# Layer norm moved into the projection stage, and half of a short filter moved from TensorE to ScalarE and VectorE

## The chip, the cores and the metric

The kernel runs on one core of one Trainium2 chip. The metric is the time of one execution in device microseconds. Before the change three runs gave a median of 2584.63 us (2580.68 to 2588.43).

## What is computed

The reference is an attention-like block with a mixture of experts behind it, for 4 sequences of 2048 tokens with 256 channels, all in float32. Only its beginning matters here:

```python
h = _layernorm(x, axis=-1) * (1 + ca) + sa
q = silu(_causal_dwconv(h @ Wq, conv_q))      # 4 taps, one filter per channel
k = silu(_causal_dwconv(h @ Wk, conv_k))
v = silu(_causal_dwconv(h @ Wv, conv_v))
beta = sigmoid(h @ Wb)                        # and sigmoid(h @ Wid + bid)
fs = _fir(v, fir_short)                       # 3 taps per channel
fl = _fir(v, fir_long)                        # 31 taps per channel
```

Behind it follow the long filter, a delta rule in chunks, the mixing of `fs`, `fl` and the delta output, and the experts. None of that is changed.

## The kernel before, in words

The program is a row of stages. Each is a block with one instruction stream per engine, and all engines meet at a barrier where one stage ends and the next begins: `setup`, `norm_inputs`, `conv_heads`, `long_filter`, `chunk_inverses`, `delta_scan`, `mix_and_experts`. Nothing orders instructions but the order in which they are written in each engine's stream and the semaphores they wait for. Every engine takes its stream strictly in that order.

The tokens are cut into 16 units of 512 (4 per sequence). `norm_inputs` works unit by unit: VectorE (DVE) takes mean and variance (`bn_stats` L312, `bn_aggr` L316, L318), GpSimd (POOL) raises the variance to the power -1/2 (L350), VectorE centers and scales (L328), TensorE (PE) turns the tile with eight transposes (L361), ScalarE (ACT) applies the modulation while it copies the result out of PSUM as `hT` (L398). TensorE then makes eight gate rows (L370), ScalarE copies them (L406), TensorE turns them back (L377) and ScalarE keeps them (L411). SyncE loads `x` and stores `hT` to `hT_d`, which a later stage reads too. At the stage's end one sigmoid runs over all gates (L416).

`conv_heads` loads `hT` again (L495) and makes, for each unit, six projection blocks of 128 channels (four of q and k, then two of v; `project`, L539). ScalarE copies each block twice: plainly into `pre` (L594) and times the last tap into `acc` (L597). VectorE adds the other three taps (`conv`, L675, three instructions per block), and ScalarE applies silu (L626). The tiles of the previous unit are meanwhile turned back to tokens on partitions: `turn_kq` (L565, four transposes) four times, and `turn_v` four times. `turn_v` makes two transposes of v (L551) and, in the same pass, the short filter as matmuls with diagonal weights: 2 channel halves times 3 taps (L555). ScalarE copies these out (`cv_k` L649, `cv_sq` L650, `cv_vf` L655), VectorE sums squares (L684), POOL makes the inverse norm (L709, L713).

All of it is written as one software pipeline by `units_ahead`: `front` does unit 0, and `body` does unit u's turns and unit u+1's projections in six slots. In slot s TensorE runs projection s, then `turn_kq` s, then `turn_v` s-1; ScalarE runs `cv_k`, `cv_sq`, the two copies of projection s, silu of block s-1 and the copy of turned v; VectorE runs the sum of squares s-1 and the filter of block s. `pj` has two buffers, so projection s waits until block s-2 has been copied out, and `acc` has three.

## Time and profile before

| what | value |
|---|---|
| median of 3 runs | 2584.63 us |
| lowest and highest run | 2580.68 and 2588.43 us |
| profiled execution: span from first to last instruction | 2587.5 us |
| profiled execution: own time | not listed apart from the span |
| busy in the span | PE 93%, PEld 64%, DVE 64%, ACT 43%, POOL 24% |
| mean granted TensorE clock | 0.946 of full speed |

The profile is one execution. PE is TensorE's matmuls, PEld its weight loads, which overlap them. A row of the timeline gives the start in us from the span's start, the duration of the merged run of equal instructions, the engine, the line, what it writes and reads, how many, and in brackets how long the engine was idle before and who ended that. Durations of neighbouring instructions overlap a little, since the next one starts before the last one's end is recorded; so the distance from one start to the next is what an instruction costs its engine when work is queued.

### The profile page before, as it was taken

Reading aid. Unit: us, or ns where it says so; the run is one execution under the profiler, and the core shown is the slowest. Engines: PE = TensorE matmul, PEld = TensorE weight load, DVE = VectorE, ACT = ScalarE, POOL = GpSimd, SP = SyncE. Lnnn points to the kernel's source line nnn. Section 1 sums busy time; section 2 is a strip of 40 time slices with the busy share of each in tenths; the row PEclk is TensorE's granted clock in tenths of the full one; section 3 lists DMA queues with packets and bytes.
Section 4 is the critical chain, followed back from the end, with each engine's and each line's share of the span. In section 5 each row is a group of like instructions: output and inputs, shape, how many; then the busy total and the mean of one; then the engine's idle time right before and its main releaser. Section 6 shows DMA issues by size and latency. Waiting matters only on the chain.

```text
span 2587.5 us, 41994 instructions
## 1 busy us (share of the span) xinstructions
PE 2394.4 (93%) x14594; PEld 1659.7 (64%) x14594; DVE 1655.0 (64%) x4354; ACT 1109.5 (43%) x2350; POOL 616.3 (24%) x417
## 2 busy tenths in 40 slices
PE   6899997667897999979999999999999999999998
PEld 4466665555676888845666666666666666666665
DVE  4487886449922566525767676667667676766675
ACT  2477876346663222224334424433443344244331
POOL 1145554031101111211312231222123132312210
PEclk9999998787667999989999999999999999999999
DMA  5447556978767767421202210220122022101000
GB/s 166 162 149 219 174 166 192 270 212 203 212 155 223 217 204 225 156 74 49 58 1 58 58 50 9 58 58 13 45 59 58 1 58 58 43 15 58 9 9 8
DMA packets 376312, 272.14 MB, mean 105 GB/s; under 512 B 199714, under 2 KB 333794, under 8 KB 373906
## 3 DMA queue, kind: packets, MB, share of 16 engines
q1 hardware_dynamic: 371474, 243.85, 33.6%
q0 software_dynamic: 4640, 25.73, 2.9%
q8 instruction: 115, 1.88, 0.3%
q14 instruction: 83, 0.68, 0.1%
HBM read 168.60 MB, written 100.93 MB: 104 GB/s over the span
## 4 chain that ended last, share of the span: by engine, by line
PE 43%; DVE 9%; issue 3%; POOL 2%; ACT 0%; DMA 0%; DVEq 0%; SPq 0%; POOLq 0%; ACTq 0%
PE mx_dn L2002 16%; PE mx_up L1988 15%; PE mx_m L1938 4%; DVE mx_acc L2316 4%; PE mx_m L1965 2%; POOL mx_rms L1894 2%; PE mx_m L1942 1%; PE mx_m L1979 1%; DVE hl L2224 1%; DVE mx_st L2214 1%; DVE hl L2199 1%; DVE hl L2188 1%; DVE mx_rms L2193 1%; PE mx_m L1973 1%; PE mx_m L1947 1%
## 5 line engine op out<-in xcount | busy, mean ns | idle before, releaser
L2316 DVE SCALAR_TENSOR_TENSOR mx_acc<-mx_dn,mx_comb,mx_acc 128x256 f32<-128x256 f32 x1024 | 424.3, 478 | 356.6 <-PE mx_dn L2002 352.7
L2002 PE MATMUL mx_dn<-mx_edn,mx_hs 128*128 128x256 f32 x2048 | 487.7, 381 | 0.0
L1988 PE MATMUL mx_up<-mx_h2T,mx_eup 128*128 128x512 f32 x1024 | 484.3, 595 | 0.0
L2002 PEld LDWEIGHTS mx_dn<-mx_edn,mx_hs 128*128 128x128 f32 x2048 | 384.4, 190 | 145.6 <-issue 91.0
L2090 ACT ACTIVATE mx_hs<-mx_up 128x512 f32<-128x512 f32 x320 | 190.8, 596 | 625.8 <-PE mx_up L1988 625.1
L1988 PEld LDWEIGHTS mx_up<-mx_h2T,mx_eup 128*128 128x128 f32 x1024 | 190.9, 190 | 156.1 <-issue 145.2
L675 DVE SCALAR_TENSOR_TENSOR cv_acc<-cv_pre,conv_w,cv_acc 128x512 f32<-128x512 f32 x288 | 215.7, 750 | 78.2 <-ACT cv_acc L597 71.3
L539 PE MATMUL cv_pj<-cv_hT,wqkv 128*128 128x512 f32 x384 | 181.8, 604 | 12.7 <-ACT cv_acc L597 7.7
L713 POOL TENSOR_TENSOR rn<-cv_ss,half_pow 128x8 f32 x64 | 127.5, 1992 | 13.2 <-POOL cv_ss L709 13.2
L1880 POOL TENSOR_TENSOR mx_st<-mx_tmp,root_pow 128x24 f32<-128x24 f32 x30 | 124.6, 4168 | 20.1 <-DVE mx_tmp L2142 20.1
L1938 PE MATMUL mx_m<-mx_hT,wr 128*128 128x512 f32 x256 | 122.2, 601 | 3.3 <-DMA mx_x<-_attn_hidden_states_dram 2.5
L1653 ACT ACTIVATE ds_U<-ds_ups 64x256 f32<-64x256 f32 x64 | 24.1, 377 | 232.2 <-PE ds_ups L1517 232.2
L2002 PEld LDWEIGHTS mx_dn<-mx_sdn,mx_hs 128*128 128x128 f32 x512 | 97.3, 190 | 40.5 <-issue 30.6
L1988 PE MATMUL mx_up<-mx_h2T,mx_sup 128*128 128x512 f32 x256 | 120.7, 605 | 2.0 <-issue 2.0
L2002 PE MATMUL mx_dn<-mx_sdn,mx_hs 128*128 128x256 f32 x512 | 121.0, 379 | 0.0
L539 PEld LDWEIGHTS cv_pj<-cv_hT,wqkv 128*128 128x128 f32 x384 | 67.6, 192 | 73.2 <-issue 54.7
L1150 PE MATMUL ci_gps<-ci_kT 64*128 64x128 f32 x768 | 84.8, 361 | 20.5 <-ACT ci_A L1229 13.2
L1575 DVE TENSOR_TENSOR ds_att<-ds_attps,upper 128x256 f32<-128x256 f32 x128 | 48.4, 420 | 84.5 <-PE ds_attps L1495 82.6
L2090 ACT ACT_TABLE_LOAD x76 | 97.5, 1283 | 7.0 <-issue 3.3
L555 PE MATMUL cv_vfps<-diag_fs,cv_vT 128*128 128x128 f32 x768 | 97.4, 277 | 0.0
L817 PE MATMUL fl_ps<-fl_toep,fl_vc 128*84 128x98 f32 x512 | 51.9, 266 | 44.9 <-DVE fl_vc L861 20.6
L555 PEld LDWEIGHTS cv_vfps<-diag_fs,cv_vT 128*128 128x128 f32 x768 | 91.9, 194 | 0.0
(292 smaller groups left out, 3998.7 us busy)
## 6 DMA issues: line engine op xcount, KB each, us to landing
kqT_d<-cv_kqc SPq DMA_DIRECT2D x16, 1024.0 KB, 8.5
vf_d<-cv_vf SPq DMA_DIRECT2D x16, 1024.0 KB, 5.4
fl_toep<-taps_d SPq DMA_DIRECT2D x32, 392.0 KB, 7.3
ds_kqT<-kqT_d SPq DMA_DIRECT2D x10, 1024.0 KB, 5.9
fl_v<-vf_d SPq DMA_DIRECT2D x8, 1216.0 KB
ci_kT<-kqT_d POOLq DMA_DIRECT2D x19, 512.0 KB, 5.7
fl_d<-fl_out POOLq DMA_DIRECT2D x8, 1029.0 KB, 7.2
xin<-_attn_hidden_states_dram SPq DMA_DIRECT2D x16, 512.0 KB, 4.3
```

The source lines that it names most:

```text
L539: ins = pe.matmul(pj[o % 2][:], m.wqkv[:, k, weight(o) * P:(weight(o) + 1) * P], hT[i][:, k, :], start=(k == 0), stop=(k == KD - 1))
L555: ins = pe.matmul(vf_ps[j % 2][:, D + k * P:D + (k + 1) * P], vT[i][:, k, c0 + t:c0 + t + P], m.diag_fs[:, k, t, :], start=(t == 0), stop= ...
L675: ins = dve.scalar_tensor_tensor(out=acc[o % 3][:], in0=pre[i][:, o, t:t + UT], scalar=m.conv_w[:, weight(o), t:t + 1], in1=acc[o % 3][:], ...
L713: pool.tensor_tensor(m.rn[:, bass.ds(u * (J * 2 * H) + j * 2 * H, 2 * H)], ss[j % 2][:], m.half_pow[:, 0:2 * H], ALU.pow).then_inc(rn_done, 1)
L817: ins = pe.matmul(ps[g % RP][0:NA, c // 4, (c % 4) * WIN:(c % 4 + 1) * WIN], vc[:, g % GH * TC + c, :], m.toep[g % RT][:, c, ::-1], start= ...
L1150: ins = pe.matmul(g_ps[n % 2][h % 2][:, h // 2 * P:(h // 2 + 1) * P], kT[k % KB][r, b, h // 2, :], kT[k % KB][r, b, h // 2, :], start=True ...
L1880: pool.tensor_tensor(std[:, :, 1, :], tmp[:, 2, part].rearrange("p (a h) -> p a h", h=H), m.root_pow[:, part].rearrange("p (a h) -> p a h" ...
L1938: pe.matmul(M[(f + 1) % 2][:], m.wr1[:, k, f * P:(f + 1) * P], hT[i][:, k, :], start=(k == 0), stop=False)
L1988: ins = pe.matmul(up_ps[x % 2][:], lhs, h2T[i][:, k, :], start=(k == 0), stop=(k == KD - 1))
L2002: ins = pe.matmul(dn_ps[(i + n) % 2][:, j, :], hs[x % 4][:, j * P:(j + 1) * P], rhs, start=(x == 0 and j % 2 == 0) or x >= NS, stop=(x >= ...
L2090: act.activation(hs[x % 4][:], up_ps[x % 2][:], ACT.Silu).then_inc(silu_done, 1)
L2316: ins = dve.scalar_tensor_tensor(out=acc[i][:, j, :], in0=dn_ps[(i + n) % 2][:, j, :], scalar=comb[i][:, j, e:e + 1], in1=acc[i][:, j, :], ...
```

## The change

`norm_inputs` is gone as a stage, with its barrier and with the second load of `hT`. Its work is put into the six slots of `conv_heads`. In `body` for unit u:

- VectorE takes the moments of unit u+3 after filter 2 and centers it, now in place in `xin`, after filter 4 (`moments`, `center`); POOL's power for it stands between the second and third inverse norm.
- TensorE turns the centered unit u+2 ahead of projection 0 (`turn_x`), makes its gate rows after projection 2 (`gate`) and turns them back after projection 4 (`gate_back`). One PSUM tile `tp` of two banks serves all three.
- ScalarE writes `hT` of unit u+2 in slot 1 (`keep_h`) and copies the gates in slots 3 and 5.

`hT` now stays in SBUF for the projections and is stored to `hT_d` by SyncE.

The short filter of the first channel half leaves TensorE. ScalarE multiplies v by the last tap into `fsT` right behind the last silu of a unit; VectorE adds the two other taps (`short`) at the beginning of its `body`; TensorE turns `fsT` with one transpose in each `turn_v`, in place of three matmuls. The second half stays as it was. Work for unit n is left out where n is beyond 15.

```diff
@@ TensorE
+            def turn_x(n, g):
+                pe.wait_ge(xn_done, n + 1)
+                if not isinstance(n, int) or n:
+                    pe.wait_ge(gcopy_done, n)
+                for k in range(KD):
+                    for j in range(J):
+                        ins = pe.transpose(tp[:, k, j * P:(j + 1) * P], xin[g % UB][:, j, k * P:(k + 1) * P], m.ident[:])
+                ins.then_inc(tp_done, 1)
+
+            def gate(n, g):
+                pe.wait_ge(h_done, n + 1)
+                for k in range(KD):
+                    ins = pe.matmul(gt, m.wgate[:, k, :], hT[g % 2][:, k, :], start=(k == 0), stop=(k == KD - 1))
+                ins.then_inc(gt_done, 1)
...
             def body(u, g, nxt):
+                n = u + 2
                 for s in range(NBLK):
+                    if exists(n) and s == 0:
+                        turn_x(n, g + 2)
                     if nxt is not None:
                         project(nxt, g + 1, s)
+                    if exists(n) and s == 2:
+                        gate(n, g + 2)
+                    if exists(n) and s == 4:
+                        gate_back(n)
...
@@ turn_v
-                for k in range(KD):
-                    for t in range(FIRS):
-                        ins = pe.matmul(vf_ps[j % 2][:, D + k * P:D + (k + 1) * P], vT[i][:, k, c0 + t:c0 + t + P],
-                                        m.diag_fs[:, k, t, :], start=(t == 0), stop=(t == FIRS - 1))
+                if j == 0:
+                    pe.wait_ge(fsT_done, u + 1)
+                pe.transpose(vf_ps[j % 2][:, D:D + P], fsT[:, c0:c0 + P], m.ident[:])
+                for t in range(FIRS):
+                    ins = pe.matmul(vf_ps[j % 2][:, D + P:2 * D], vT[i][:, 1, c0 + t:c0 + t + P], m.diag_fs[:, 1, t, :],
+                                    start=(t == 0), stop=(t == FIRS - 1))
@@ ScalarE, silu
+                if o == NBLK - 1:
+                    act.wait_ge(silu_done, u * NBLK + (NBLK + 2))
...
+                    act.activation(fsT[:], vT[i][:, 0, FIRS - 1:], ACT.Identity, scale=m.fs_w[:, 0, FIRS - 1:FIRS])\
+                        .then_inc(tap_done, 1)
@@ ScalarE, body
+                    if exists(n) and s == 1:
+                        keep_h(n, g + 2)
+                    if exists(n) and s == 3:
+                        keep_gT(n)
+                    if exists(n) and s == 5:
+                        keep_gates(n)
@@ VectorE
+            def short(u, g):
...
+                dve.wait_ge(tap_done, u + 1)
+                dve.wait_ge(vhalo_done, u + 1)
+                dve.scalar_tensor_tensor(out=fsT[:], in0=vT[i][:, 0, 1:1 + UT], scalar=m.fs_w[:, 0, 1:2], in1=fsT[:],
+                                         op0=ALU.mult, op1=ALU.add).then_inc(tap_step, 1)
...
             def body(u, g, nxt):
+                n = u + 3
+                short(u, g)
                 for s in range(NBLK):
                     if 1 <= s < J + 1:
                         reduce_sq(u, s - 1)
                     if nxt is not None:
                         conv(nxt, g + 1, s)
+                    if exists(n) and s == 2:
+                        moments(n, g + 3)
+                    if exists(n) and s == 4:
+                        center(n, g + 3)
@@ SyncE
-                sp.wait_ge(pj_done, u * NBLK + NBLK)
-                sp.dma_start(hT[i][:], m.hT_d[bass.ds(u, 1)].squeeze(0)).then_inc(h_in[i], 16)
+            def load(u):
+                if u < NU:
+                    sp.wait_ge(tp_done, u - UB + 1)
+                    sp.dma_start(xin[u % UB][:], x_v[u]).then_inc(x_in[u % UB], 16)
+
+            def put_h(u):
+                sp.wait_ge(h_done, u + 1)
+                sp.dma_start(m.hT_d[u], hT[u % 2][:]).then_inc(h_store[u % 2], 16)
@@ build
-EARLY = [inputs, conv_heads]
+EARLY = [setup, conv_heads]
```

How the orders stand. First TensorE where one unit's last projection (5) is followed by the next `body`. L539 is `project`, L565 `turn_kq`. Before:

```order
L539 MATMUL cv_pj<-cv_hT,wqkv 128x512 [waits cv_pre_done]
L539 MATMUL cv_pj<-cv_hT,wqkv 128x512
L535 ISA
L537 ISA [waits cv_h_in0]
L539 MATMUL cv_pj<-cv_hT,wqkv 128x512 [waits cv_pre_done]
L539 MATMUL cv_pj<-cv_hT,wqkv 128x512
L561 REGISTER_ALU
L563 ISA [waits cv_silu_done]
L565 MATMUL cv_kqps<-ident,cv_kqc 128x128 [waits cv_sq_done]
```

The same place now, where L387 is `project`, L425 `turn_x`, L415 `turn_kq`:

```order
L387 MATMUL cv_pj<-cv_hT,wqkv 128x512 [waits cv_pre_done]
L387 MATMUL cv_pj<-cv_hT,wqkv 128x512
L420 REGISTER_ALU
L425 MATMUL ln_tp<-ident,xin 128x128 [waits ln_gcopy_done,ln_xn_done]
L425 MATMUL ln_tp<-ident,xin 128x128 x7
L385 ISA [waits ln_h_done]
L387 MATMUL cv_pj<-cv_hT,wqkv 128x512 [waits cv_pre_done]
L387 MATMUL cv_pj<-cv_hT,wqkv 128x512
L411 REGISTER_ALU
L413 ISA [waits cv_silu_done]
L415 MATMUL cv_kqps<-ident,cv_kqc 128x128 [waits cv_sq_done]
```

Eight transposes that wait for VectorE's centering stand now ahead of projection 0 and of all that follows it.

Then TensorE in slot 2. Before (L551 and L555 are `turn_v`):

```order
L539 MATMUL cv_pj<-cv_hT,wqkv 128x512 [waits cv_pre_done]
L539 MATMUL cv_pj<-cv_hT,wqkv 128x512
L563 REGISTER_ALU
L565 MATMUL cv_kqps<-ident,cv_kqc 128x128 [waits cv_sq_done]
L565 MATMUL cv_kqps<-ident,cv_kqc 128x128 x3
L551 MATMUL cv_vfps<-ident,cv_vT 128x128 [waits cv_vfe_done]
```

Now (L431 is `gate`):

```order
L387 MATMUL cv_pj<-cv_hT,wqkv 128x512 [waits cv_pre_done]
L387 MATMUL cv_pj<-cv_hT,wqkv 128x512
L431 MATMUL ln_tp<-cv_hT,wgate 8x512 [waits ln_h_done]
L431 MATMUL ln_tp<-cv_hT,wgate 8x512
L413 REGISTER_ALU
L415 MATMUL cv_kqps<-ident,cv_kqc 128x128 [waits cv_sq_done]
L415 MATMUL cv_kqps<-ident,cv_kqc 128x128 x3
```

The gate matmuls stand between projection 2 and the turn of q and k.

Last, VectorE from the centering over the unit's end (L652 `center`, L612 the filter, L622 and L625 `short`), as it is now:

```order
L652 TENSOR_SCALAR xin<-xin,ln_mv,ln_rstd 128x256 [waits ln_rstd_done]
L652 TENSOR_SCALAR xin<-xin,ln_mv,ln_rstd 128x256 x3
L606 REGISTER_ALU
L612 SCALAR_TENSOR_TENSOR cv_acc<-cv_pre,conv_w,cv_acc 128x512 [waits cv_pre_done]
L611 ISA
L612 SCALAR_TENSOR_TENSOR cv_acc<-cv_pre,conv_w,cv_acc 128x512 [waits cv_conv_step]
L611 REGISTER_ALU
L612 SCALAR_TENSOR_TENSOR cv_acc<-cv_pre,conv_w,cv_acc 128x512 [waits cv_conv_step]
L622 SCALAR_TENSOR_TENSOR cv_fsT<-cv_vT,fs_w,cv_fsT 128x512 [waits cv_vhalo_done,cv_tap_done]
L625 SCALAR_TENSOR_TENSOR cv_fsT<-cv_vT,fs_w,cv_fsT 128x512 [waits cv_tap_step]
```

Before, only filters and sums of squares stood in this stream; the centering and the two taps of `short` are new in it.

## Rows read from the trace of the kernel before

**Rows 1.** The page's first line.
```profile
span 2587.5 us, 41994 instructions
```
**Rows 2.** Windows: stretch, its length, busy us of each engine, granted clock, DMA.
```profile
60.00:80.00 20.00, 16.84 (x91) 9.41 (x89) 14.80 (x61) 9.80 (x20) 5.14 (x5) 1.00 0.71 232
...
220.00:300.00 80.00, 78.27 (x402) 51.71 (x403) 65.28 (x93) 63.81 (x134) 42.32 (x33) 1.00 0.63 192
```
**Rows 3.** Timeline, norm stage's first unit, and unit 0's last silu in the projection stage.
```profile
32.28 1.40 DVE L312 BATCH_NORM_STATS2 ln_stats<-xin 128x6 f32<-128x256 f32 x4 [7.95 <-PEq L43]
...
34.36 1.40 DVE L312 BATCH_NORM_STATS2 ln_stats<-xin 128x6 f32<-128x256 f32 x4
...
41.37 3.58 PE L370 MATMUL ln_gt<-hT,wgate 128*8 128x512 f32 x4 [1.67 <-ACT hT L398]
...
140.04 0.63 ACT L626 ACTIVATE cv_vT<-cv_acc 128x512 f32<-128x512 f32 x1 [1.60 <-DVE cv_acc L675]
```
**Rows 4.** Timeline, one warm unit of the norm stage.
```profile
62.06 1.88 PE L370 MATMUL ln_gt<-hT,wgate 128*8 128x512 f32 x4 [0.78 <-ACT hT L398]
...
64.89 1.05 PE L377 MATMUL ln_gp<-back,ln_gT 9*128 9x8 f32 x8
65.08 1.38 DVE L328 TENSOR_SCALAR xn<-xin,ln_mv,ln_rstd 128x256 f32<-128x256 f32 x4 [0.27 <-PE ln_tp L361]
65.16 1.45 ACT L398 ACTIVATE hT<-ln_tp,ln_modb 128x512 f32<-128x512 f32 x2 [0.47 <-PE ln_tp L361]
```
**Rows 5.** Timeline, TensorE in one slot of the projection stage.
```profile
204.16 1.88 PE L539 MATMUL cv_pj<-cv_hT,wqkv 128*128 128x512 f32 x4
...
205.88 0.60 PE L565 MATMUL cv_kqps<-ident,cv_kqc 128*128 128x128 f32 x4
...
206.54 1.50 PE L555 MATMUL cv_vfps<-diag_fs,cv_vT 128*128 128x128 f32 x12
...
207.88 1.88 PE L539 MATMUL cv_pj<-cv_hT,wqkv 128*128 128x512 f32 x4
```
**Rows 6.** Timeline, VectorE in the same slot.
```profile
205.50 0.68 DVE L684 TENSOR_REDUCE cv_ss<-cv_sq 128x8 f32<-128x512 f32 x1
...
206.09 2.31 DVE L675 SCALAR_TENSOR_TENSOR cv_acc<-cv_pre,conv_w,cv_acc 128x512 f32<-128x512 f32 x3
...
208.32 0.68 DVE L684 TENSOR_REDUCE cv_ss<-cv_sq 128x8 f32<-128x512 f32 x1
```
**Rows 7.** Timeline, ScalarE and VectorE over a unit's end, and unit 15's last silu.
```profile
408.48 0.63 ACT L626 ACTIVATE cv_vT<-cv_acc 128x512 f32<-128x512 f32 x1 [1.88 <-DVE cv_acc L675]
...
409.31 0.38 ACT L649 ACTIVATE cv_k<-cv_kqps 128x256 f32<-128x256 f32 x1
...
411.28 2.33 DVE L675 SCALAR_TENSOR_TENSOR cv_acc<-cv_pre,conv_w,cv_acc 128x512 f32<-128x512 f32 x3 [2.83 <-ACT cv_acc L597]
...
427.60 0.63 ACT L626 ACTIVATE cv_vT<-cv_acc 128x512 f32<-128x512 f32 x1 [1.88 <-DVE cv_acc L675]
```
**Rows 8.** Timeline, TensorE after two idle stretches.
```profile
428.28 0.44 PE L551 MATMUL cv_vfps<-ident,cv_vT 128*128 128x128 f32 x2 [3.42 <-ACT cv_vT L626]
...
428.55 2.67 PE L555 MATMUL cv_vfps<-diag_fs,cv_vT 128*128 128x128 f32 x12
...
561.91 3.73 PE L1150 MATMUL ci_gps<-ci_kT 64*128 64x128 f32 x32 [2.40 <-DMA ci_kT<-kqT_d]
```
**Rows 9.** Windows of TensorE: stretch, length, busy us, granted clock, DMA.
```profile
430.00:432.00 2.00, 2.00 (x11) 0.50 0.40 121
...
517.00:521.00 4.00, 2.56 (x29) 1.00 1.14 271
```
**Rows 10.** Timeline, POOL's add of the inverse norm beside VectorE's filter, and without one.
```profile
206.25 0.64 POOL L709 TENSOR_TENSOR cv_ss<-cv_ss,l_eps 128x8 f32<-128x8 f32 x1
...
207.07 2.04 POOL L713 TENSOR_TENSOR rn<-cv_ss,half_pow 128x8 f32 x1 [0.18 <-POOL cv_ss L709]
...
432.04 0.20 POOL L709 TENSOR_TENSOR cv_ss<-cv_ss,l_eps 128x8 f32<-128x8 f32 x1
```

More of the change, by code:

```diff
@@ L459, in conv_heads @@
         ss = [sb(f"cv_ss{i}", [P, 2 * H]) for i in two]
+        xin, x_in = m.xin, m.x_in
+        stats = sb("ln_stats", [P, J, 6])
+        mv = [sb(f"ln_mv{i}", [P, J, 2]) for i in two]
+        rstd = [sb(f"ln_rstd{i}", [P, J]) for i in two]
+        modb = sb("ln_modb", [P, 4])
+        pad = sb("ln_pad", [P, 1])
+        gT = sb("ln_gT", [2 * H + 1, UT])
+        tp = ctx.enter_context(nc.psum_tensor("ln_tp", [P, KD, UT], F32))
+        gt, gp = tp[0:2 * H, 0, :], tp[:, 1, 0:J * 8]
         pj = [psum(f"cv_pj{i}") for i in two]
@@ L462, in conv_heads @@
         kq_ps = [psum(f"cv_kqps{i}") for i in two]
-        h_in = [sem(f"cv_h_in{i}") for i in two]
+        h_store = [sem(f"ln_h_store{i}") for i in two]
+        vec_step = sem("ln_vec_step")
+        mod_step = sem("ln_mod_step")
+        var_done = sem("ln_var_done")
+        rstd_done = sem("ln_rstd_done")
+        xn_done = sem("ln_xn_done")
+        tp_done = sem("ln_tp_done")
+        h_done = sem("ln_h_done")
+        one_done = sem("ln_one_done")
+        gt_done = sem("ln_gt_done")
+        gT_done = sem("ln_gT_done")
+        g_done = sem("ln_g_done")
+        gcopy_done = sem("ln_gcopy_done")
         store = [sem(f"cv_store{i}") for i in two]
@@ L505, in put @@
                 sp.dma_start(m.vf_d[rows].rearrange("j p c -> p j c"), vf[i][:]).then_inc(store[i], 16)
-            load(0, 0)
-            load(1, 1)
+            for u in two:
+                load(u + UB)
+                put_h(u)
             for u in range(2, NU):
-                load(u, u % 2)
+                load(u + UB)
+                put_h(u)
                 if u - 2 < RT0:
@@ L657, in _ @@
             units_ahead(act, front, body)
+            act.wait_ge(gcopy_done, NU)
+            act.activation(m.gates[:], m.gates[:], ACT.Sigmoid).then_inc(gcopy_done, 1)
+            act.wait_ge(gcopy_done, NU + 1)
         @block.vector
@@ L705, in _, with scale_x, front, body @@
             pool.wait_ge(m.v_zero, 2 * B)
-            def body(u):
+            pool.memset(gT[:], 1.0).then_inc(one_done, 1)
+            def scale_x(n, g):
+                i = g % 2
+                pool.wait_ge(var_done, n + 1)
+                pool.tensor_tensor(rstd[i][:], mv[i][:, :, 1], m.half_pow[:, 0:J], ALU.pow).then_inc(rstd_done, 1)
+            def front(u, g):
+                for n in range(3):
+                    scale_x(n, n)
+            def body(u, g, nxt):
                 for j in range(J):
+                    if j == 2 and exists(u + 3):
+                        scale_x(u + 3, g + 3)
                     pool.wait_ge(red_done, u * J + (j + 3))
@@ L714, in body @@
                                        m.half_pow[:, 0:2 * H], ALU.pow).then_inc(rn_done, 1)
-            with pool.Fori(0, NU) as u:
-                body(u)
+            units_ahead(pool, front, body)
 def load_toep(sp, m, g):
```

254 lines of the change are left out of this document (90 added, 164 removed).

## The prediction

> **What bounds the kernel now.** I read the page's first line for the span the sum is made against, 2587.5 us [rows 1]; it lies 2.9 us above the median of the runs, so I carry the difference over to 2584.6. About 0.3% (7.8 us) is what a measurement of this kernel can tell from no change. Then I read the windows by stage. The norm stage begins at about 32 us [rows 3]; in it no engine is full, TensorE with 16.84 of 20 us the most [rows 2]. In the projection stage TensorE is busy 78.27 of 80 us, VectorE 65.28, ScalarE 63.81 [rows 2]: TensorE bounds it. The last silu of unit 0 starts at 140.04, that of unit 15 at 427.60 [rows 3, 7]: 287.56 / 15 = 19.17 us per unit. I call the end of a unit's last filter C; it is 0.04 before such a silu. Stages before and behind are not touched, and the stage behind starts when this one ends, so what C of unit 15 moves by, the whole moves by.
>
> **What an instruction costs its engine** is the distance between starts. TensorE: a projection 205.88 - 204.16 = 1.72; the 18 short matmul records of one q/k turn and one v turn take 207.88 - 205.88 = 2.00, 0.111 each, so the q/k turn (4) 0.44, the v turn (14) 1.56 [rows 5]. Per unit 6 x 1.72 + 4 x 0.44 + 4 x 1.56 = 18.3, and about 0.9 of waiting makes the 19.17. VectorE: a filter 208.32 - 206.09 = 2.23, a sum of squares 0.59 [rows 6]; per unit 6 x 2.23 + 4 x 0.59 = 15.7.
>
> **What goes.** The norm stage and its barrier, the load of hT, and what ramps up at the projection stage's start. The first unit still has to be normed before its first projection: moments 2.08 (34.36 - 32.28) [rows 3], POOL's memsets and its power (estimate: ready at 36.1), centering 1.38 [rows 4], transposes at TensorE's low clock 2.0, hT 1.45 [rows 4]: 41.1. A projection at half clock is 3.5 (the gate matmuls, of the same width, took 3.58 cold and 1.88 warm [rows 3, 4]), copies 1.2: first filter at 45.9. Six filters 13.4, one set of moments 2.1, a table load and the first gates' round trip 2.2 (estimate): C of unit 0 at 63.6, where it was 140.0. **-76.4 us**, give or take 3. The hT stores and x loads move to SyncE's queue in the projection stage. Each is issued a unit or more before it is needed, and one 0.5 MB transfer more per unit beside a DMA share of 0.63 [rows 2] costs nothing; if that cover were gone, ScalarE would wait for a store in slot 0 or 1, some us per unit (in the range).
>
> **What each unit gains in work.** TensorE: the v turn has 3 transposes and 6 records in place of 2 and 12, 9 x 0.111 = 1.0, four times: -2.2. Added: eight transposes 0.88, gate matmuls 1.72 (1.88 recorded, like a projection), the turn back 1.0 [rows 4, 5]. 18.3 - 2.2 + 3.6 = 19.7. VectorE: `short` two of the three thirds of a filter 1.5, moments 2.08, centering 1.38: 15.7 + 5.0 = 20.7. So VectorE has now more to do than TensorE ever had, and the order matters. ScalarE: hT 1.45, gates 0.6, the tap 0.6, on 63.81 / 80 x 19.17 = 15.3: about 18, not the bound.
>
> **The loop that sets the period.** X is the end of a centering. TensorE's queue has eight transposes that wait for X at the head of the next `body`, and all else queues behind them. From X: 0.05 + 0.88 (transposes) + 1.72 + 0.44 + 1.72 + 0.44 (projections and turns 0 and 1) + 1.0 (v turn 0) + 1.72 (projection 2) + 1.72 (gate) + 0.60 (q/k turn 2 until its end [rows 5]) = 10.3. ScalarE takes that turn's copies before those of projection 2, so filter 2 starts 1.97 later (from the copy `cv_k` at 409.31 to the filter at 411.28 it is the same four instructions [rows 7]): X + 12.3. Then VectorE goes without a pause: filter 2.23, moments 2.08, sum 0.59, filter 2.23, sum 0.59, filter 2.23, centering 1.38 = 11.3. **Period 23.6** at full clock. The other loop, over ScalarE at the unit's end, is: C, silu, tap, halos until 0.83 + 0.6 later, then 1.97 to the next filter 0 [rows 7], so VectorE idles 3.4 less 1.5 of `short`, and 0.8 more before filters 1 and 2; 20.7 + 2.7 = 23.4. It lies just under the first. The `short` wait itself (v turn 0 needs C + 2.9) is met as TensorE comes there at X + 5.2, which is C + 3.0.
>
> **The clock.** In this loop TensorE has done projection 5 at X + 20.0 (10.1, then 9.6 of work, 0.3 for its end) and then waits for the next X, 3.5 us. The trace shows what such a wait does: after 3.42 us idle at the end of this very stage twelve records took 2.67 in place of 1.50 [rows 5, 8], and the granted clock was still 0.50 between 430 and 432 [rows 9], that is 1.2 GHz of 2.4. Price 1.17 and half of some 0.8 further us, 1.6, and it falls on the first part of the loop above, in which every TensorE us counts. The Trainium skill, "TensorE: Matmul & The Clock Gate", section "HAM oscillation — how this bites in real kernels", speaks against this change in the same way: a kernel whose groups of matmuls wait long enough for something else starts every group cold again, and pays the change of clock once per group. The trace agrees for one such wait and has no series of them. Bounds per unit: 0 (after the wait of 2.40 that ended at 561.91 the records were slow [rows 8], but between 517 and 521, with 1.44 of 4 us idle, the clock stayed 1.00 [rows 9]) and 1.8 (half of the 3.6 us at the low clock). I take 1.3, four falls in five units. With 0.1 for the jump of the hardware loop the period is **25.05**.
>
> **The sum.** 13 units (bodies 0 to 12) have all work: 13 x (25.05 - 19.17) = +76.4. Body 0 starts late, because the centering of unit 2 and the gates of unit 1 lie between C and its transposes: +5.3, and it is cold, +1.6. Body 13 has no moments but still transposes: +3.7; body 14 has neither: +0.2. The end behind C of unit 15: v turn 0 waits 2 us more, four turns are 0.56 shorter, the gates' sigmoid lies beside the last store: 0 (bounds -2 and +2). -76.4 + 76.4 + 6.9 + 3.9 = +10.8, so 2584.6 + 10.8 = **2595 us**, slower by 0.4%. Its own range, with 0.5 us either way per unit and the start's 3: 2586 to 2604. What is saved is a whole stage, and what is paid is 6 us in every unit.
>
> **The rivals.**
> - The clock does not fall: period 23.75, body 0 and 13 without the cold part: -76.4 + 13 x 4.58 + 5.3 + 2.0 + 0.2 = -9.4, **2575 us, faster**. For it: in the norm stage TensorE was busy 84% with clock 1.00 [rows 2], and it will be as busy here. Against it: there the waits were 0.8 us each [rows 4], here it is one of 3.5. It decides from the point at which the wait in front of the transposes stays well under 2.4 us. Chance 0.22.
> - Orders overlap better than I worked out, and VectorE's sum plus one unavoidable wait for silu and tap binds: 20.7 + 1.4 = 22.1 per unit, 21 us under the rival above: **2553 us**. Against it: each step of the loop is a queue in order. Chance 0.08.
> - VectorE's centering or its taps wait for POOL. POOL's power of 2.04 us [rows 10] runs when the centering comes due. At present POOL pays and VectorE doesn't: its add took 0.64 beside filters and 0.20 without [rows 10], a filter 2.31 to 2.33 in both [rows 6, 7]. If the centering had to wait half of that power, +1.0 in the loop: 13 x 1.0 on the forecast, **2608 us**. Other waits in the loop give the same. Chance 0.15. By the Trainium skill, "SBUF — State Buffer", section "Who interferes with whom", VectorE and POOL share a port pair under an exclusive lock, and an instruction that comes second waits until the first is done; by that rule a centering behind the power waits. The trace has centering beside POOL's power only with the centering first, so it doesn't show this case.
>
> Chances: the forecast's case 0.55. Faster by over 0.3% (below 2577): most of the second case's lower part, 0.13, and 0.07: 0.20. Within (2577 to 2592): 0.09 and a third of the likeliest, 0.19: 0.28. Slower: 0.36 + 0.15, 0.52 with rounding. The range for 8 in 10 reaches from below the case of the full clock to the third rival: 2568 to 2608.
>
> **What would show it.** In the changed profile: the first projection near 41 us and C of unit 0 near 64; a distance of about 25 us between silus of last blocks; TensorE idle some 3.5 us in front of the `ln_tp` transposes of each unit, released by VectorE's centering; a granted clock near 0.93 in the stage, where it was 1.00; VectorE idle between a unit's last filter and `short`, and in front of filters 1 and 2. It is wrong in its centre if that idle time in front of the transposes is short, if the clock stays at 1.00, or if the last silu of unit 15 comes before 427 us.

## The result, and the profile after

The changed kernel takes **2601.28 us** (median of 5 executions, 2595.69 to 2609.27) where the kernel before takes 2584.63 (5 executions, 2580.45 to 2588.43): ratio 1.0054, 95% interval 1.0029 to 1.0079, slower. The profiled execution took 2602.37 us. The forecast was 2595, range 2568 to 2608.

The page's first line answers to [rows 1]:

```profile
span 2600.3 us, 41119 instructions
```

Timeline of the changed kernel, answering to [rows 3, 7]: start and duration in us, engine, line, what it writes and reads, and in brackets the idle time before it with the one that ended it. First transposes, first projection, last silu of unit 0 and of unit 15.

```profile
38.50 1.97 PE L425 MATMUL ln_tp<-ident,xin 128*128 128x128 f32 x8 [6.47 <-DVE xin L652]
...
42.06 1.22 PE L387 MATMUL cv_pj<-cv_hT,wqkv 128*128 128x512 f32 x1 [1.59 <-ACT cv_hT L542]
...
64.59 0.63 ACT L513 ACTIVATE cv_vT<-cv_acc 128x512 f32<-128x512 f32 x1 [1.61 <-DVE cv_acc L612]
...
438.06 0.63 ACT L513 ACTIVATE cv_vT<-cv_acc 128x512 f32<-128x512 f32 x1 [1.61 <-DVE cv_acc L612]
```

Unit 0 is finished 75.45 us earlier than before (64.59 against 140.04), unit 15 is 10.46 us later (438.06 against 427.60). So the 15 distances between units grew by 85.9 us, from 287.6 to 373.5. The rest of the span's difference, 12.8 - 10.5, arises in stages that the change does not touch. Between the medians the difference is 16.65 us; the 3.9 beyond the spans' 12.8 come from where each profiled span stands against its kernel's median (2.9 above it before, 1.0 below it after). The distances between last silus, from unit 0 on, are 32.0, 26.5, 27.0, 25.3, 27.2, 23.9, 24.0, 23.9, 27.3, 23.9, 24.0, 23.9, 23.8, 21.6, 19.2.

One of the undisturbed units on TensorE (timeline, 224 to 248):

```profile
224.24 1.09 PE L425 MATMUL ln_tp<-ident,xin 128*128 128x128 f32 x8 [3.64 <-DVE xin L652]
225.17 1.88 PE L387 MATMUL cv_pj<-cv_hT,wqkv 128*128 128x512 f32 x4
...
227.33 1.88 PE L387 MATMUL cv_pj<-cv_hT,wqkv 128*128 128x512 f32 x4
...
242.73 1.88 PE L387 MATMUL cv_pj<-cv_hT,wqkv 128*128 128x512 f32 x4
248.25 0.98 PE L425 MATMUL ln_tp<-ident,xin 128*128 128x128 f32 x7 [3.64 <-DVE xin L652]
```

TensorE has nothing queued between its sixth projection, at 242.73, and the next transposes, at 248.25: they are at the head of the next body and wait for VectorE's centering. VectorE over the same unit:

```profile
222.81 1.37 DVE L652 TENSOR_SCALAR xin<-xin,ln_mv,ln_rstd 128x256 f32<-128x256 f32 x4
224.10 2.32 DVE L612 SCALAR_TENSOR_TENSOR cv_acc<-cv_pre,conv_w,cv_acc 128x512 f32<-128x512 f32 x3
227.73 0.75 DVE L622 SCALAR_TENSOR_TENSOR cv_fsT<-cv_vT,fs_w,cv_fsT 128x512 f32<-128x512 f32 x1 [1.31 <-ACT cv_fsT L518]
...
236.90 2.33 DVE L612 SCALAR_TENSOR_TENSOR cv_acc<-cv_pre,conv_w,cv_acc 128x512 f32<-128x512 f32 x3 [0.51 <-ACT cv_acc L484]
239.14 1.40 DVE L640 BATCH_NORM_STATS2 ln_stats<-xin 128x6 f32<-128x256 f32 x4
...
246.82 1.38 DVE L652 TENSOR_SCALAR xin<-xin,ln_mv,ln_rstd 128x256 f32<-128x256 f32 x4
```

Between the last wait, ended at 236.90 by a copy of ScalarE, and the centering at 246.82, VectorE runs without a pause. From the centering's end (224.2) to filter 2 at 236.90 it is 12.7 us, from there to the end of the next centering 11.3: the loop that the prediction called X, 24.0 us. One POOL power of 2.04 us began at 221.56, before the centering at 222.81 (timeline of POOL):

```profile
221.56 2.04 POOL L707 TENSOR_TENSOR rn<-cv_ss,half_pow 128x8 f32 x1 [0.18 <-POOL cv_ss L703]
```

A second view is the windows (stretch, length, busy us of PE, PEld, DVE, ACT, POOL with counts, granted clock, DMA):

```profile
80.00:160.00 80.00, 69.02 (x297) 40.88 (x296) 62.30 (x117) 54.28 (x114) 29.94 (x28) 0.89 0.50 157
160.00:240.00 80.00, 66.07 (x316) 39.15 (x315) 65.18 (x122) 58.32 (x123) 31.70 (x29) 1.00 0.59 184
240.00:320.00 80.00, 65.67 (x311) 38.34 (x309) 65.97 (x128) 56.77 (x118) 34.05 (x31) 1.00 0.49 159
```

Against [rows 2] TensorE fell from 78.27 to 65.67 busy us in 80, and no other engine is full. The clock was down only in the first units, until about 152 us; over the whole stretch from 64.6 to 438 us windows give 0.97. What a fall costs is seen at 120.86 (timeline): from the transposes to the second projection 6.03 us, where it was 3.09 at 224.24; the wait ahead of both is the same.

```profile
120.86 1.97 PE L425 MATMUL ln_tp<-ident,xin 128*128 128x128 f32 x8 [3.65 <-DVE xin L652]
122.62 3.62 PE L387 MATMUL cv_pj<-cv_hT,wqkv 128*128 128x512 f32 x4
...
126.89 1.93 PE L387 MATMUL cv_pj<-cv_hT,wqkv 128*128 128x512 f32 x4
```

The two units of 27.2 and 27.3 us are not cold (a cold unit is one in which the clock fell). There ScalarE does nothing for 3.5 us at the head of its loop; the releaser "issue" means that it waited for nothing the profile shows. First row: the changed kernel. The row under it is from the kernel before, at its own jump.

```profile
180.37 0.38 ACT L577 ACTIVATE cv_k<-cv_kqps 128x256 f32<-128x256 f32 x1 [3.51 <-issue]
```

```profile
217.89 0.38 ACT L649 ACTIVATE cv_k<-cv_kqps 128x256 f32<-128x256 f32 x1 [0.38 <-issue]
```

The DMA view of the changed kernel from 176 to 184 has four transfers of instructions in it (queue, kind: packets, MB, share of 16 engines), some 8 KB each; the kernel before has one such transfer from 204 to 224.

```profile
q14 instruction: 4, 0.03, 1.5%
```

The hardware loop goes three times over a group of four units and jumps back twice, and there are two such units. ScalarE's loop has 270 instructions in the changed kernel and 229 in the kernel before.

### The profile page after: what moved, and what is told of

It is laid out like the page before. It is cut to its first block, busy times and chain, and to the rows that moved or that the text cites. A ratio compares the mean times of both kernels' runs of the same rounds, so it can differ in the third digit from the quotient of the medians.

```text
span 2600.3 us, 41119 instructions
## 1 busy us (share of the span) xinstructions
PE 2384.1 (92%) x14274; PEld 1644.1 (63%) x14274; DVE 1680.1 (65%) x4386; ACT 1117.4 (43%) x2367; POOL 592.2 (23%) x416
## 4 chain that ended last, share of the span: by engine, by line
PE 43%; DVE 9%; issue 2%; POOL 2%; ACT 0%; DMA 0%; DVEq 0%; SPq 0%; POOLq 0%; ACTq 0%
PE mx_dn L1995 16%; PE mx_up L1981 15%; PE mx_m L1931 4%; DVE mx_acc L2309 4%; PE mx_m L1958 2%; POOL mx_rms L1887 2%; PE mx_m L1935 1%; PE mx_m L1972 1%; DVE hl L2217 1%; DVE mx_st L2207 1%; DVE hl L2192 1%; DVE hl L2181 1%; DVE mx_rms L2186 1%; PE mx_m L1966 1%; PE mx_m L1951 1%
## 5 line engine op out<-in xcount | busy, mean ns | idle before, releaser
L612 DVE SCALAR_TENSOR_TENSOR cv_acc<-cv_pre,conv_w,cv_acc 128x512 f32<-128x512 f32 x288 | 216.0, 751 | 59.4 <-ACT cv_acc L484 52.6
L387 PE MATMUL cv_pj<-cv_hT,wqkv 128*128 128x512 f32 x384 | 187.2, 613 | 6.9 <-ACT cv_acc L484 5.3
L707 POOL TENSOR_TENSOR rn<-cv_ss,half_pow 128x8 f32 (+1 forms) x64 | 120.7, 1886 | 10.0 <-POOL cv_ss L703 8.8
L1143 PE MATMUL ci_gps<-ci_kT 64*128 64x128 f32 x768 | 94.2, 398 | 13.6 <-ACT ci_A L1222 6.7
L387 PEld LDWEIGHTS cv_pj<-cv_hT,wqkv 128*128 128x128 f32 x384 | 68.5, 198 | 58.7 <-issue 50.1
L1143 PEld LDWEIGHTS ci_gps<-ci_kT 64*128 64x128 f32 x768 | 75.3, 272 | 27.1 <-ACT ci_A L1222 11.2
L1587 DVE TENSOR_SCALAR ds_U<-ds_ups 64x256 f32<-64x256 f32 x64 | 27.4, 428 | 91.5 <-PE ds_ups L1527 91.5
```

The costliest lines, as they stand in the source:

```text
L387: ins = pe.matmul(pj[o % 2][:], m.wqkv[:, k, weight(o) * P:(weight(o) + 1) * P], hT[i][:, k, :], start=(k == 0), stop=(k == KD - 1))
L612: ins = dve.scalar_tensor_tensor(out=acc[o % 3][:], in0=pre[i][:, o, t:t + UT], scalar=m.conv_w[:, weight(o), t:t + 1], in1=acc[o % 3][:], ...
L707: pool.tensor_tensor(m.rn[:, bass.ds(u * (J * 2 * H) + j * 2 * H, 2 * H)], ss[j % 2][:], m.half_pow[:, 0:2 * H], ALU.pow).then_inc(rn_done, 1)
L1143: ins = pe.matmul(g_ps[n % 2][h % 2][:, h // 2 * P:(h // 2 + 1) * P], kT[k % KB][r, b, h // 2, :], kT[k % KB][r, b, h // 2, :], start=True ...
```

## The experiments

Three questions were open: is the loop over the centering what sets the distance, or VectorE's sum; what is the stall at the jump; and which half of the change costs what. Each kernel was timed in 3 rounds against the kernel before on the same chip. "Last silu" is that of unit 15, 427.60 before and 438.06 in the changed kernel.

### ScalarE without a jump

```diff
-            units_ahead(act, front, body)
+            front(0, 0)
+            for u in range(NU):
+                body(u, u % UB, u + 1 if u < NU - 1 else None)
```

> The changed kernel with ScalarE's hardware loop over pairs of units written out as sixteen units in a row, so that ScalarE never jumps; no other engine and no instruction's order is touched. Theory (the jump costs): in the changed kernel two units (27.16 and 27.27 us between last silus, where their neighbours at the same full clock have 23.9) hold a stall of 3.5 us that ScalarE shows behind 'issue' at the head of its loop. Without the jump both fall to about 23.9: -6.6 us, so about 2594.7 us beside 2601.3 for the changed kernel, +0.4% on the kernel before, last silu of unit 15 near 431.4. Rival (the stall is something that recurs wherever the loop's first body stands, as table loads or a DMA of the stage): both units stay at 27.2, no difference, 2601. Third case: instructions fetched in a row stall as well, spread over all units: slower, over 2605.

(The loop covers groups of four units, not pairs.) Measured: 2588.3 us (10 executions) beside 2586.0 for the kernel before, ratio 1.0002, 95% interval 0.9984 to 1.002. That is 0.5% under the changed kernel, and the two ratios' intervals do not touch (1.0029 to 1.0079 there). Timeline and windows:

```profile
426.34 0.63 ACT L513 ACTIVATE cv_vT<-cv_acc 128x512 f32<-128x512 f32 x1 [1.60 <-DVE cv_acc L614]
```

```profile
100.00:200.00 100.00, 85.34 (x405) 50.10 (x403) 83.95 (x157) 75.49 (x158) 39.63 (x36) 1.00 0.53 165
200.00:300.00 100.00, 85.35 (x404) 49.73 (x404) 85.02 (x158) 74.81 (x157) 42.66 (x40) 1.00 0.55 175
```

The distances are 23.9 from the third unit on, without exception: the jump did cost 2 x 3.3 = 6.6 us. The last silu is 11.7 us earlier; the other 5 are mostly falls of the clock, of which this execution had one in bodies 1 to 12 where the changed kernel had three. The time lies 6 us under the 2594.7 expected, presumably for the same reason.

### The kernel before with a longer loop on ScalarE

```diff
+                    if s == 3:
+                        act.wait_ge(halo_done, 1)
+                        act.wait_ge(vhalo_done, 1)
+                        act.wait_ge(pre_done, 1)
+                        act.wait_ge(silu_done, 1)
+                        act.wait_ge(pj_done, 1)
...
```

> The kernel before, with 20 waits on already satisfied semaphores added in each unit on ScalarE, 40 in its loop: 269 instructions in it where the kernel before has 229 and the changed one 270. No work is added. Theory (the length of ScalarE's loop decides whether its jump stalls): two jumps at some 3.0 to 3.3 us each show up in the distances of the silus of units 5/6 and 9/10 or wherever the loop turns, and fetches of instructions appear at those moments: +6 to +7 us, 2591 us. Twenty waits by themselves cost ScalarE some 1 us per unit beside 3.8 us of idle time it has, so 0 to +4 us more. Rival (the length is harmless, the stall of the changed kernel has to do with what its loop does): 2584 to 2588 us and no fetches there.

Measured: 2593.97 us, ratio 1.0027 (1.0008 to 1.0046). In the profiled execution the last silu stood at 427.57, no distance changed by more than 0.3, and no instructions were fetched at the jumps. So 269 instructions did not stall, and the theory in its plain form fell. The 0.3% stay unexplained: the profiled execution took 2586.17 us, 8 under the median of its kernel, so its trace does not show where the others lost time (executions of the kernel before alone spread from 2578 to 2601 in the three sessions).

### The same loop, begun at another place

```diff
+            def front_(u, g):
+                front(u, g)
+                for _ in range(10):
+                    act.wait_ge(pj_done, 1)
+                    act.wait_ge(pre_done, 1)
+                    act.wait_ge(halo_done, 1)
+                    act.wait_ge(vhalo_done, 1)
+                    act.wait_ge(silu_done, 1)
+
-            units_ahead(act, front, body)
+            units_ahead(act, front_, body)
```

> The changed kernel with 50 waits on satisfied semaphores on ScalarE between unit 0's projections and its loop, carried out once (25 instructions); the loop itself keeps its 270 instructions. Before this run: without a jump the stall is gone, 270 instructions stall (changed kernel, and the one with the centering early), 269 (the kernel before with waits added) and 265 do not. Theory A (what counts is where the loop begins and ends against the 8 KB pieces in which instructions are fetched): the shift moves the loop into a better place, both stalls of 3.3 us go, units of 27.2 fall to 23.9, no fetches behind the jumps: 2601.3 - 6.6 = 2595 us, or to 2589 as in the kernel without the jump if the clock falls less often as well. Theory B (the number of instructions alone, with a limit between 269 and 270): stalls and fetches stay, 2601 us.

Measured: 2593.9 us beside 2589.75, ratio 1.0017 (0.9994 to 1.0039); the interval overlaps that of the changed kernel, so it is the trace that decides. At the first jump ScalarE waits for TensorE and no longer for "issue", and at the second it does not pause at all. First jump, timeline:

```profile
174.75 0.38 ACT L577 ACTIVATE cv_k<-cv_kqps 128x256 f32<-128x256 f32 x1 [1.19 <-PE cv_kqps L415]
```

The distances over the two jumps were 25.4 (a cold one) and 24.0, and between 161 and 409 us ScalarE fetched nothing. The last silu stood at 432.88, 5.2 us earlier than in the changed kernel. The loop is as long as in the changed kernel. So what stalls is not the length alone but how a loop of this length lies: the instructions were fetched in pieces of 8 KB (in the kernel without a jump one piece about every 70 us from 200 us on, some 140 instructions of that stream by an estimate from its 746 instructions for 16 units), and in the changed kernel four pieces came behind each jump. 25 idle instructions ahead of the loop cure it, here and in the last experiment below. The Trainium skill, "Advanced Engine Details and Errata", section "ISA Cache", gives an engine's instruction cache as 32 KB with only two lines of 256 instructions. That a loop of some 270 may or may not fit agrees with this; the pieces seen here are half of its lines.

This run shows something else as well. TensorE's wait in front of the transposes is the 3.64 to 3.72 us of the changed kernel, and the full-clock distance is the same 23.9, and yet the clock fell in five of bodies 1 to 12 (25.3 to 25.6 us), two of them late in the stage. One of them, timeline:

```profile
364.54 1.97 PE L425 MATMUL ln_tp<-ident,xin 128*128 128x128 f32 x8 [3.64 <-DVE xin L661]
```

Its profiled execution was the fastest of ten, 6.7 us under the median.

### Norm inside, short filter back on TensorE

```diff
-                if j == 0:
-                    pe.wait_ge(fsT_done, u + 1)
-                pe.transpose(vf_ps[j % 2][:, D:D + P], fsT[:, c0:c0 + P], m.ident[:])
-                for t in range(FIRS):
-                    ins = pe.matmul(vf_ps[j % 2][:, D + P:2 * D], vT[i][:, 1, c0 + t:c0 + t + P], m.diag_fs[:, 1, t, :],
-                                    start=(t == 0), stop=(t == FIRS - 1))
+                for k in range(KD):
+                    for t in range(FIRS):
+                        ins = pe.matmul(vf_ps[j % 2][:, D + k * P:D + (k + 1) * P], vT[i][:, k, c0 + t:c0 + t + P],
+                                        m.diag_fs[:, k, t, :], start=(t == 0), stop=(t == FIRS - 1))
...
-                short(u, g)
```

> The changed kernel with the short filter fully back on TensorE (no tap on ScalarE, no short on VectorE, v turn with two times six records again); the norm stays inside the projections' turns. Theory of the prediction (the loop over the centering sets the period, TensorE's time from the centering to filter 2 counts in full, VectorE's sum does not): the v turn in that loop grows by 0.56 us, so at full clock a unit takes 23.9 + 0.5 = 24.4 us and the wait of TensorE in front of the transposes shrinks from 3.64 to about 1.9 us (3 more v turns of 0.56 lie beside it). 13 units x 0.5 = +6.5 us less what fewer falls of the clock give back (5 falls at up to 3 us each): 2594 to 2608 us. Rival (VectorE's sum of work bounds the changed kernel): VectorE has 1.5 us less in each unit, -20 us: 2581 us.

Measured: 2595.26 us, ratio 1.0026 (1.0008 to 1.0045), last silu 438.90 in a profiled execution that was the slowest of eleven (2613.83), so this silu is not to be set against the median. At full clock the units are 24.45 us apart. Timeline and window:

```profile
294.29 1.09 PE L423 MATMUL ln_tp<-ident,xin 128*128 128x128 f32 x8 [1.96 <-DVE xin L633]
```

```profile
200.00:300.00 100.00, 92.07 (x471) 57.51 (x470) 76.00 (x145) 69.91 (x146) 38.72 (x36) 0.98 0.51 164
```

VectorE was given 1.5 us less to do per unit and the distance grew by 0.56, one v turn: the loop over the centering, with TensorE's time from X to filter 2 in it, is the bound. VectorE's sum of work is not. Yet in this execution the clock fell in every third unit (26.15 us), though the wait in front of the transposes was only 1.96 to 2.05.

### Centering one slot earlier

```diff
-                    if exists(n) and s == 2:
+                    if exists(n) and s == 1:
                         moments(n, g + 3)
-                    if exists(n) and s == 4:
+                    if exists(n) and s == 3:
                         center(n, g + 3)
...
-                    if j == 2 and exists(u + 3):
+                    if j == 1 and exists(u + 3):
                         scale_x(u + 3, g + 3)
```

> The changed kernel with the moments of the unit ahead one slot earlier on VectorE (behind filter 1 in place of 2), POOL's power one turn earlier, and the centering behind filter 4's slot in place of the last: the same instructions in another order. Theory (loop over the centering): the centering comes some 5 us earlier against the transposes, the wait of TensorE in front of them (3.64 us) goes, that loop falls under the other one, over the unit's end (silu, tap, halos, short, first filters), which I put at 22.9 to 23.4 us. So 0.5 to 1 us less in each of 13 units, 7 to 13 us, and some of the falls of the clock less, up to 5 x 1.6: 2583 to 2594 us; no wait of over 1 us in front of the ln_tp transposes. Rival (VectorE's sum of work with its unavoidable waits is the bound): the period stays at 23.9, 2598 to 2602 us.

Measured: 2586.72 us, ratio 0.9994 (0.9971 to 1.0017), last silu 426.07. The distances are 22.9 and 23.4 at full clock, 23.9 with a fall, and 26.8 and 26.6 where ScalarE's loop jumps (its 270 instructions lie as they did, and the clock falls behind the stall). Timeline of TensorE, one unit:

```profile
307.51 1.06 PE L425 MATMUL ln_tp<-ident,xin 128*128 128x128 f32 x8 [0.17 <-DVE xin L652]
...
315.39 0.33 PE L403 MATMUL cv_vfps<-ident,cv_fsT 128*128 128x128 f32 x1 [1.75 <-DVE cv_fsT L625]
```

The wait of 3.64 is gone, and the other loop of the prediction, put at 23.4, is what is left: TensorE now waits for `short`.

### The short filter's move alone

On the kernel before, with the norm stage kept:

```diff
-                for k in range(KD):
-                    for t in range(FIRS):
-                        ins = pe.matmul(vf_ps[j % 2][:, D + k * P:D + (k + 1) * P], vT[i][:, k, c0 + t:c0 + t + P],
-                                        m.diag_fs[:, k, t, :], start=(t == 0), stop=(t == FIRS - 1))
+                if j == 0:
+                    pe.wait_ge(fsT_done, u + 1)
+                pe.transpose(vf_ps[j % 2][:, D:D + P], fsT[:, c0:c0 + P], m.ident[:])
...
+                short(u, g)
```

> The kernel before with the second part of the change alone: the short filter of the first half of the channels by ScalarE's tap and VectorE's two steps, one transpose in the v turn; the norm stage stays. TensorE per unit 18.3 - 2.2 = 16.1 us, VectorE 15.7 + 1.5 = 17.2. Theory (what binds then is the loop over the unit's end: silu, tap, halos, short, first filters, each waiting for the one ahead): 19.2 to 19.9 us per unit where the kernel before has 19.17, 0 to +10 us, 2585 to 2595. Rival (TensorE's sum of work still bounds, as it did): -2.2 us in each of 15 units, -33 us, 2552.

Measured: 2602.99 us beside 2589.75, ratio 1.0045 (1.0026 to 1.0065), last silu 441.47. TensorE has 2.2 us less work in each unit, and a unit takes 20.15 us on average in place of 19.17: more than either theory allowed. Timeline of TensorE and window:

```profile
242.44 0.33 PE L559 MATMUL cv_vfps<-ident,cv_fsT 128*128 128x128 f32 x1 [1.75 <-DVE cv_fsT L700]
...
243.39 3.46 PE L543 MATMUL cv_pj<-cv_hT,wqkv 128*128 128x512 f32 x4
```

```profile
160.00:240.00 80.00, 72.11 (x302) 43.74 (x302) 68.38 (x96) 63.27 (x129) 37.19 (x32) 0.91 0.57 174
```

The direction was right, since silu, tap, `short` and filter 0 now follow one another. What was left out is the clock: it fell in 11 of the 15 units behind that wait, and the projection behind it took 3.46 us for 1.88. The four units at full clock lie 19.2 to 19.3 us apart, the lower end of what the theory gave: there the chain takes back the 2.2 us that TensorE was spared, and no more. The loss beyond that is the clock's. In this order this half of the change is a loss by itself.

### Norm inside, centering early, short filter on TensorE

Both edits above in one kernel: the v turn of before, and moments, power and centering one slot earlier.

> The changed kernel with the short filter back on TensorE and with moments, power and centering one slot earlier: both edits that were tried alone. The loop over the centering is gone by the earlier order, the loop over tap and short by their absence. Left is TensorE's sum of work, 18.3 + 3.6 = 21.9 us, with some 0.5 us of short waits: 22.4 us per unit where the run with the early centering alone had 22.9 and 23.4, so some 0.7 us less in 13 units, -9 us; and without the two stalls of ScalarE's jump (265 instructions in its loop) -6.6 us: 2586.7 - 15.6 = 2571 us, 0.6% under the kernel before. Rival (VectorE's sum and its waits at the unit's end still bind at 22.9): 2580 us. Third case (TensorE's clock falls in many units): 2585 us or more.

Measured: **2569.58 us** (8 executions, 2564.66 to 2574.82) beside 2589.75, ratio 0.9923 (0.9898 to 0.9948): faster than both kernels. Windows, and the last silu:

```profile
160.00:240.00 80.00, 79.19 (x408) 49.74 (x407) 65.09 (x120) 62.01 (x129) 36.60 (x31) 1.00 0.62 194
240.00:320.00 80.00, 79.20 (x417) 51.14 (x417) 68.03 (x136) 61.79 (x128) 40.36 (x35) 1.00 0.54 172
```

```profile
408.62 0.63 ACT L511 ACTIVATE cv_vT<-cv_acc 128x512 f32<-128x512 f32 x1 [1.87 <-DVE cv_acc L604]
```

TensorE is busy 79.2 of 80 us, the distances are 22.3 to 22.9 (expected 22.4), the clock is 1.00 from 74 us to the last silu, and there is no stall at the jump. The last silu is 19 us earlier than before, as much as the whole kernel gains.

### One statistics instruction more on VectorE

On the kernel without ScalarE's jump:

```diff
+        spare = sb("ln_spare", [P, 6])
...
                 dve.wait_ge(x_in[g % UB], (n - g % UB) * 4 + 16)
+                dve.bn_stats(spare[:], xin[g % UB][:, 0, :])
```

> The kernel without ScalarE's jump (its units at full clock are 23.89 us apart) with one more statistics instruction of 0.35 us per unit on VectorE ahead of the moments, its result unused. It lies in the loop over the centering. Both theories: period at full clock 24.2, TensorE's wait in front of the transposes 3.64 + 0.35 = 4.0 us. Theory A (how long TensorE waits decides whether its clock falls): a wait of 3.64 was followed by full clock for 328 us on end, one of 4.0 in a few units falls or not at all alike; without falls 13 x 0.35 = +4.6 us, 2588.3 + 4.6 = 2593 us, granted clock 1.00 from the third unit on. Theory B (the steady clock was a matter of the distance of 23.89 itself, since at 24.45 and a wait of only 1.96 it fell in every third unit): it falls again in one unit of three to five, at 1.7 us each: 3 to 5 falls, +10 us, 2596 to 2600, granted clock 0.98 or less in windows of 80 us in which it is now 1.00.

Measured: 2619.74 us (4 executions) beside 2588.5, ratio 1.0117 (1.0079 to 1.0155), last silu 458.49. A third of a microsecond more in each of 13 units made the stage 32 us longer than in the run it was added to. The distances of bodies 1 to 12 are 25.5 to 27.2 throughout. Timeline and window:

```profile
297.53 0.42 DVE L642 BATCH_NORM_STATS2 ln_spare<-xin 128x6 f32<-128x256 f32 x1
```

```profile
306.97 1.09 PE L426 MATMUL ln_tp<-ident,xin 128*128 128x128 f32 x8 [3.97 <-DVE xin L656]
...
332.88 1.97 PE L426 MATMUL ln_tp<-ident,xin 128*128 128x128 f32 x8 [3.97 <-DVE xin L656]
```

```profile
200.00:300.00 100.00, 86.86 (x371) 51.04 (x371) 77.20 (x149) 68.57 (x143) 33.28 (x33) 0.90 0.50 161
```

The clock fell in every unit. Theory B had the direction, with a third of the size; A fell. The size of the wait alone does not decide, since the kernel with the filter back on TensorE had falls behind 1.96 us. And the steady clock of the kernel without a jump is itself no fixed property of a wait of 3.64 us and a distance of 23.9, since the kernel with the loop begun elsewhere had five falls at both. This run cannot say whether 3.97 instead of 3.64 or the changed distance brought the falls back.

### The v turn one projection later

With the early centering and the 25 idle instructions of above:

```diff
-                    if 1 <= s < J + 1:
-                        turn_v(u, g, s - 1)
+                    if 2 <= s < J + 2:
+                        turn_v(u, g, s - 2)
...
-                    if 1 <= s < J + 1:
-                        act.wait_ge(vf_done, u * J + s)
+                    if 2 <= s < J + 2:
+                        act.wait_ge(vf_done, u * J + (s - 1))
```

> The changed kernel (short filter shared as in the change) with the centering early, the 50 waits ahead of ScalarE's loop that take away the stalls of its jump, and every v turn and its eviction one projection later. With the centering early TensorE waited 1.75 us per unit in front of v turn 0 for VectorE's short, with the projections queued behind it. Theory (that wait is part of the loop over the unit's end): it goes, and what is left is VectorE's work 20.7 + 1.3 for the tap + 0.6 before filters: 22.6 us per unit instead of 22.9 and 23.4; 13 x 0.5 = -6.5 and -6.6 for the stalls: 2586.7 - 13 = 2573.5 us. Rival (VectorE's chain of silu, tap, short and first filter holds the distance, and TensorE's wait only ran beside it): the distance stays at 22.9 to 23.2, -6.6 alone, 2580 us.

Measured: 2588.33 us, ratio 1.0004 (0.9981 to 1.0027), last silu 425.54. Distances 23.3 to 24.2, longer than the 22.9 and 23.4 without this edit and than either theory had, and the time misses both. The wait for `short` went, and one behind it came (timeline):

```profile
314.49 1.98 PE L387 MATMUL cv_pj<-cv_hT,wqkv 128*128 128x512 f32 x4 [2.21 <-ACT cv_acc L484]
```

TensorE, ahead by one turn, runs into the two buffers of `pj`: the projection waits for ScalarE's copy of block 0, which itself comes behind silu and tap. And the clock fell in eight of bodies 1 to 12. So the wait for `short` was not what held the distance: once it is gone, another wait on the same chain of ScalarE and VectorE takes its place. What the edit and the falls each cost was not separated; the gain from the stalls was given back.

## Why the prediction was right, and where it was not

The total is right: 2601.3 us lies 6 above the forecast, in its own range of 2586 to 2604, and slower as said. In the stage itself the profiled executions moved by 10.46 us for a forecast of 10.8; the 6 us arise outside it and between executions. Point by point:

- **What goes.** Unit 0 was done (C) at 64.55, forecast 63.6; -75.45 for -76.4. First projection at 42.06 for 41.1. Right.
- **The loop over the centering.** 23.9 us at full clock for a forecast of 23.6 to 23.75, TensorE's wait 3.64 for 3.5. The two experiments that touched it confirmed its structure: one v turn more in it made it longer by just that (24.45), and an earlier centering took it away and left the second loop (22.9 and 23.4 for 23.4).
- **The queue moves at no cost.** From 100 to 440 us the list of waits holds none for a DMA. Right.
- **Body 0 and the last bodies.** Body 0 took 32.0, for 25.05 + 6.9; body 13 took 21.6 for 22.9, body 14 19.2 for 19.4. Right within 1.3.
- **The clock: "I take 1.3, four falls in five units".** This step failed, in both factors. In the profiled execution the clock fell in three of the twelve bodies 1 to 12 and stayed at 1.00 in the others behind the same wait of 3.64; where it fell it cost 1.4 to 3.1 us where 1.6 was put, since the transposes and projection 0 ran at 1.2 GHz nearly throughout (6.03 us for 3.09 up to projection 1). Together 7 us where 12 x 1.3 = 15.6 was forecast. The mean clock from unit 0's last silu to unit 15's was 0.97, not near 0.93, and from 152 us on it stayed at 1.00, which the prediction itself had listed as a sign of being wrong in its centre. The number of falls is not a property of the code alone: five executions of the changed kernel had mean clocks of 0.930 to 0.938. The rule cited from the Trainium skill ("TensorE: Matmul & The Clock Gate", section "HAM oscillation — how this bites in real kernels"), that such a kernel starts every group cold, was borne out only behind 3.97 us. Behind the same 3.64 us the clock fell in three, one and five of bodies 1 to 12 (changed kernel, no jump, loop begun elsewhere), and 1.96 was enough for every third unit.
- **"0.1 for the jump of the hardware loop".** This failed too: 3.3 us at each of the two jumps, 6.6 us, shown by the run without a jump and the run with the loop begun elsewhere. No row of the kernel before hinted at it, because its loop did not stall.

These two errors cancel. Bodies 1 to 12 took 300.6 us, 25.05 each, which is the forecast to the second decimal: 12 x 23.9 = 286.8, 7.2 for falls, 6.6 for jumps. The structure was understood; the agreement of the total is in part luck. Of the rivals, "the clock does not fall" comes closest in the run without a jump, at full clock from the third unit on; the loop begun elsewhere mends the stall as well and had five falls, so it is not a settled state. The run without a jump had its last silu 1.3 us before that of the kernel before, where that rival had 9.4, because body 0 took 33.1 us for 29.05, one more unit was cold (25.3), and the full-clock distance is 23.9 for 23.75. "VectorE's sum binds" was wrong: with 1.5 us less on VectorE the distance grew by 0.56. POOL did not hold up the centering: it began at 222.81, with POOL's power running since 221.56, and took 1.37 us against 1.38 in [rows 4]. So the port rule of "SBUF — State Buffer", section "Who interferes with whom", in the Trainium skill was not seen to act on this pair, and the third rival's mechanism did not occur. The page ties its lock to VectorE's two-port modes and to instructions with two inputs in SBUF, a condition that the prediction left out; whether this centering runs in such a mode is not shown. The rival could also have been weighed from the trace of before. The prediction says that this trace has the centering beside POOL's power only with the centering first. In the very unit of [rows 4] it is the other way round: the power began at 64.89, the centering at 65.08, and it took its 1.38 us. That power is the shorter one, of 1.01 us:

```profile
64.89 1.01 POOL L350 TENSOR_TENSOR ln_rstd<-ln_mv,half_pow 128x4 f32<-128x4 f32 x1 [3.60 <-DVE ln_mv L318]
```

What the prediction did not do was to price the two halves of the change apart. The norm inside the turns costs little even in this order (1.0026) and gains with the centering one slot earlier (0.9923). The short filter's move costs by itself (1.0045), because TensorE is spared 2.2 us and then waits for the longer chain, and its clock falls behind that wait.

## What to carry to other kernels

When a stage is folded into another one, look for the step whose result heads the next round's queue on the busiest engine, and place it a slot earlier than its data seem to ask: here that one shift turned a loss of 0.3% into a gain of 0.8%. Moving work off the bounding engine gained nothing here, since the work comes back to it through a chain of three engines at the unit's end; count the chain first, and allow for the clock, which can fall behind the wait that the chain leaves. And when an added instruction makes a loop longer, look at the first instruction behind its jump in the new trace: a stall with no releaser there, with instructions fetched beside it, was removed here by moving where the loop lies.

## What the runs showed of the hardware

- A hardware loop of 270 instructions on ScalarE stalled 3.3 us at each jump, with four fetches of 8 KB beside it; the same 270 instructions behind 25 idle ones did not stall, in two kernels, nor did 269, 265 or 229 in others. VectorE's loop of 281 instructions in the changed kernel showed no such stall.
- TensorE's clock in a periodic loop does not follow the length of its wait. Behind 3.64 us in each unit it stayed at 1.00 for over 280 us with units 23.9 us apart, in two kernels; in a third with the same wait and distance it fell in five of twelve units. At 24.45 apart and 1.96 us it fell in every third unit; in the kernel with the short filter's move alone, behind 1.75 us, in 11 of 15; at 3.97 us in every unit, and then 0.35 us of added work per unit cost 32 us. Which property of the loop decides is open. A time of such a loop can therefore not be carried over to a neighbour that differs by a few tenths.
